# Spreading the second direction's input projection, its convolution and the next image's token embedding over other scan steps

## The chip, the cores and the metric

One core of one Trainium2 chip. The metric is the device time of one launch in microseconds (us), the median of the runs. One execution was taken by the profiler; its trace is what the rows below come from.

## What is computed

For each of 32 images of 224 x 224 x 3 and a text of 77 tokens, one layer of an early-fusion model. T = 1 + 196 + 77 = 274 tokens of C = 192 features.

```python
h = concat([cls, patches(x / 255) @ W + b]) + pos_emb        # 197 tokens, patch length 768
h = concat([h, txt], axis=1)                                  # 274 tokens
h = h + attn(layernorm(h))                                    # two Mamba blocks, forward and backward
h = h + ffn(layernorm(h))                                     # a transformer block

def mamba(x, ...):                        # once on x, once on x reversed in time
    xi, z = split(x @ in_proj.T)          # 384 + 384 features
    xc = silu(causal_dwconv(xi, 4 taps))
    dt_lo, B, C = split(xc @ x_proj.T)    # 12 + 16 + 16
    dt = softplus(dt_lo @ dt_w.T + dt_b)
    h_t = exp(dt_t * A) * h_(t-1) + dt_t * u_t * B_t          # 384 features x 16 states
    y = (h_t . C_t + u * D) * silu(z)
    return y @ out_proj.T
```

The mixer ends in r = x + fwd + bwd and a layernorm. The transformer block has 12 heads of 16 features and an MLP of 768. The first 16 images ("large") go through attention and MLP once; for the last 16 ("small") attention and MLP outputs are gated sums of three variants with masked heads and channels, which costs more matmuls and adds.

## The kernel before

Features lie on partitions, tokens along the free axis; everything is fp32. The five engines each have a program of their own, written by hand, and wait for each other by semaphores. The selective scan is cut into 12 half units per image: q = 0 to 5 is the first direction (d = 0), 6 to 11 the second, each half unit a tile of 128 partitions (16 states x 8 features) by 8 x 274. For each q, VectorE multiplies the loaded dt*u rows with B (`input_product`, L1073), runs one long TENSOR_TENSOR_SCAN (`scan`, L1084) and multiplies with C (`output_product`, L1090); ScalarE makes the decays by eight exps (`exps`, L832); TensorE sums over the states into `y_ps` (`sum_states`, L476 and L480), and VectorE gates the sum (`gate_unit`, L1099). dt and dt*u go through DRAM to be broadcast over partitions: SyncE writes them (`write_rows`) and reads them back (`read_half`) in a fixed order.

The order of all work is a table of gaps. `step(b, f, e, a)` is one turn of the loop: it has 2 x GAPS = 36 gaps, three for each q, and in it four images are under way. Image b is being scanned. Image f = b - 1 goes through output projection, the second layernorm and attention (`fine...` functions, with its own gap count 0 to 35), image e = b - 2 through its MLP and last sum (the same functions, gap count 36 to 45, in the first ten gaps of the step). Image a = b + 1 is prepared (`fronts...` functions). The same gap number on every engine stands for the same place in the schedule, but each engine runs through its own list as its waits allow. In this text gap g of the second direction is also called gap 18 + g.

Fronts, before: in the first half of the step (d = 0) the second direction of image b is prepared, in the second half (d = 1) the first direction of image a. In each half:

- gaps 0 to 5: `in_proj` (L516), six column blocks j of 128, two matmuls each, into the one PSUM bank `a_ps`; ScalarE's `xz_copy` (L855) empties it one gap later, j = 0 to 2 into `xi`, j = 3 to 5 into `zs[d]`.
- VectorE's `conv` (L1138 and L1142, four taps for one j) at CONV_GAPS; ScalarE's `silu` (L860 and L861, between two table loads) at gap 8.
- `x_proj_mm` (L526) and its copy at gap 10; `dt_mm` (L536) with `dt_parts` (L873 to L879, Abs, Relu, Exp, Ln) at gaps 11 to 13, `dt_sum` (L1149 and L1152) on VectorE one gap later; `c_spread` and `c_copy` at 14, `b_spread` at 15.

In the first half also the token embedding of image a: 12 matmuls `tok` (L492, gaps 6 and 7), `tok_add` (L1123, gap 7), the mean over features `a_mean_mm` (L468) and VectorE's `centre` (L1104, gap 8), ScalarE's `squares` (gap 8), `a_var_mm` (L468) and `rstd` (gap 9), and VectorE's `scale_by` that makes `xn` (L1109, gap 10). Everything of the fronts that TensorE makes except B goes through the bank `a_ps`, so its order is a strict sequence of matmuls and copies.

Of the image f, the gaps named below are: `residual` (L1157) at gap 4, which waits for `out_proj` (L556); `add_mixer` at 7; `affine` (L1116) at 10; q, k and v matmuls (L581, L606) at 11 and 12; from gap 12 on 18 slots of scores (L621) with their row maxima on VectorE one gap later (L1178) and turned scores (L629) with their exp on ScalarE (L924); `q_with_maxima` (L595, L598) at 15, 20 and 26; sums of attention inverted on ScalarE (L936, L938) and divided on VectorE (L1183) at 24, 30 and 33; `proj` (L654) at 33. Of image e: fc1 (L675) at gaps 2 and 3, gelu (L951) at 4, fc2 (L686) at 5 and 6, for small images its second and third variant at 8, `add_mlp` (L1187 or L1192) at 7 and `last_sum` (L1187, L1196, L1238) at 9.

How a gap is gone through, here on VectorE:

```python
if gap % 3 == 0: output_product(b, q - 1)
if gap % 3 == 1: scan(b, q)
if gap % 3 == 2: input_product(b, q + 1)
if gap % 6 == 2: gate_unit(b, q // 2 - 1)
for part in endings(d, gap, f, e): fine(*part)
fronts(b, d, a, gap)
```

## Time and profile before

| what | before |
|---|---|
| median of 3 runs | 5700.33 us (5692.26 to 5709.53) |
| the profiled execution | 5727.32 us |
| its span | 5725.5 us |
| VectorE (DVE) busy | 4944.8 us, 86% |
| TensorE (PE) busy | 4406.4 us, 77% |
| ScalarE (ACT) busy | 3172.3 us, 55% |
| DMA, mean of the 16 engines | 72.2% |
| granted TensorE clock, mean | 0.799 |

The span is the stretch from the first to the last instruction that the profiler saw. A timeline row gives start, duration, engine, line, operation, out<-in, shapes and count, and in brackets how long the engine had idled before it and what released it; rows of one kind that follow each other are merged, and on PE the count takes weight loads and matmuls together. The granted clock is a share of 2.4 GHz; 0.5 is the level of 1.2 GHz.

### The profile page before, as it was taken

The numbers are of one execution on the slowest core, as the hardware profiler recorded it, in microseconds if no ns is written. First come the engines' busy times: TensorE is split into PE (matmuls) and PEld (weight loads), VectorE is DVE, ScalarE is ACT, GpSimd is POOL, SyncE is SP. The second block draws the span as 40 slices with busy tenths as digits, with TensorE's granted clock in tenths as the row PEclk, the third lists the DMA queues.
The fourth block names the chain that finished last, engine by engine and source line by source line (L and its number), as shares of the span: only waits on it lengthen the run. The fifth ranks groups of instructions, "written<-read, shape, count | busy, mean of one in ns | idle before, by whom it ended". The sixth has DMA issues, their size and how long they took to land.

```text
span 5725.5 us, 69728 instructions
## 1 busy us (share of the span) xinstructions
PE 4406.4 (77%) x23852; PEld 2476.2 (43%) x23852; DVE 4944.8 (86%) x3712; ACT 3172.3 (55%) x6914; POOL 1.5 (0%) x9
## 2 busy tenths in 40 slices
PE   3577778777777877777778787788778877787877
PEld 2244444444344444444444444444445444444433
DVE  4999998999999899999998988888987889888971
ACT  2455555555565555555556655555555655556642
POOL 0000000000000000000000000000000000000000
PEclk7677888887788878877888878887877878888876
DMA  5877787778778777877786786777766677676840
GB/s 143 206 170 172 175 198 179 177 172 188 178 164 192 182 178 170 194 176 164 178 191 162 168 186 149 165 165 163 169 152 163 159 178 162 155 176 163 178 101 3
DMA packets 182843, 953.92 MB, mean 167 GB/s; under 512 B 26557, under 2 KB 76157, under 8 KB 84042
## 3 DMA queue, kind: packets, MB, share of 16 engines
q1 hardware_dynamic: 182442, 948.83, 72.2%
q8 instruction: 220, 3.60, 0.3%
q14 instruction: 181, 1.48, 0.1%
HBM read 888.14 MB, written 60.60 MB: 166 GB/s over the span
## 4 chain that ended last, share of the span: by engine, by line
PE 37%; DVE 36%; issue 14%; DMA 7%; ACT 5%; DVEq 1%; SPq 0%; ACTq 0%; POOL 0%; POOLq 0%
DVE hs L1084 15%; DVE hs L1090 6%; DVE hs L1073 5%; PE f_ps L675 4%; DMA h<-in_txt 3%; PE a_ps L516 3%; DVE neg_max L1178 3%; PE f_ps L639 3%; PE f_ps L686 2%; PE f_ps L629 2%; PE y_ps L480 2%; PE f_ps L556 2%; PE a_ps L526 2%; PE f_ps L581 2%; DVE xc L1142 2%
## 5 line engine op out<-in xcount | busy, mean ns | idle before, releaser
L1084 DVE TENSOR_TENSOR_SCAN hs<-decay,hs 128x2192 f32<-128x2192 f32 x384 | 1810.5, 4715 | 27.6 <-ACT decay L832 27.5
L832 ACT ACTIVATE decay<-decay,a_cols 128x273 f32<-128x273 f32 x3072 | 1369.0, 511 | 0.4
L1090 DVE TENSOR_TENSOR hs<-hs,c_s 128x2192 f32<-128x2192 f32 x384 | 933.5, 2431 | 56.0 <-issue 56.0
L1073 DVE TENSOR_TENSOR hs<-hs,b_ps 128x2192 f32<-128x2192 f32 x384 | 930.4, 2423 | 17.1 <-DMA hs<-dtu_rows 17.1
L924 ACT ACTIVATE hid<-f_ps 92x1096 f32<-92x1096 f32 x288 | 310.9, 1079 | 649.4 <-PE f_ps L629 649.1
L480 PE MATMUL y_ps<-hs,y_pick 128*32 128x274 f32 x6144 | 554.5, 490 | 55.4 <-DVE hs L1090 55.4
L516 PE MATMUL a_ps<-xn,w_in_s 96*128 96x274 f32 x1536 | 514.6, 463 | 98.0 <-ACT zs L855 50.5
L1178 DVE TENSOR_REDUCE neg_max<-f_ps 92x4 f32<-92x1096 f32 x288 | 371.5, 1290 | 185.9 <-PE f_ps L621 185.9
L629 PE MATMUL f_ps<-hid 32*92 32x274 f32 x1536 | 189.5, 573 | 339.5 <-DVE neg_max L1178 329.8
L516 PEld LDWEIGHTS a_ps<-xn,w_in_s 96*128 96x128 f32 x1536 | 319.2, 219 | 275.7 <-ACT zs L855 77.6
L480 PEld LDWEIGHTS y_ps<-hs,y_pick 128*32 128x32 f32 x6144 | 185.4, 127 | 374.8 <-issue 241.8
L581 PE MATMUL f_ps<-cen,w_qk_s 96*128 96x274 f32 x768 | 257.3, 471 | 90.2 <-DVE cen L1116 55.5
L1142 DVE SCALAR_TENSOR_TENSOR xc<-xi,inner_s,xc 128x274 f32<-128x274 f32 x576 | 289.9, 504 | 20.1
L675 PE MATMUL f_ps<-cen,fc_s 96*128 96x274 f32 (+2 forms) x960 | 292.4, 456 | 4.1 <-DVE cen L1116 3.1
L686 PE MATMUL f_ps<-hid,fc_s 128*96 128x274 f32 x1152 | 287.3, 399 | 7.1 <-ACT hid L951 6.0
L639 PE MATMUL f_ps<-hid,v_s 92*32 92x274 f32 x2304 | 237.3, 567 | 55.4 <-ACT hid L924 33.5
L629 PEld LDWEIGHTS f_ps<-hid 32*92 32x92 f32 x1536 | 64.3, 202 | 451.2 <-DVE neg_max L1178 309.2
L621 PE MATMUL f_ps<-hid 32*92 32x274 f32 x1536 | 169.9, 518 | 86.3 <-ACT hid L924 47.3
L675 PEld LDWEIGHTS f_ps<-cen,fc_s 96*128 96x128 f32 (+2 forms) x960 | 194.5, 212 | 92.2 <-ACT hid L944 30.6
L944 ACT ACTIVATE hid<-f_ps,fc_b_s 128x274 f32<-128x274 f32 x384 | 181.5, 489 | 93.5 <-PE f_ps L675 92.8
L581 PEld LDWEIGHTS f_ps<-cen,w_qk_s 96*128 96x128 f32 x768 | 152.5, 216 | 185.9 <-DVE cen L1116 66.5
L686 PEld LDWEIGHTS f_ps<-hid,fc_s 128*96 128x96 f32 x1152 | 188.2, 165 | 94.5 <-issue 11.5
(149 smaller groups left out, 5927.9 us busy)
## 6 DMA issues: line engine op xcount, KB each, us to landing
decay<-dt_rows SPq DMA_DIRECT2D x384, 1096.0 KB, 9.0
hs<-dtu_rows SPq DMA_DIRECT2D x384, 1096.0 KB, 12.8
dt_rows<-dt SPq DMA_DIRECT2D x192, 137.0 KB, 10.0
dtu_rows<-dtu SPq DMA_DIRECT2D x192, 137.0 KB, 9.8
xp<-in_patches SPq DMA_DIRECT2D x32, 588.0 KB, 19.5
out<-h SPq DMA_DIRECT2D x32, 205.5 KB, 2.2
h<-in_txt SPq DMA_DIRECT2D x32, 57.8 KB, 11.7
w_in_s<-in_w_in SPq DMA_DIRECT2D x1, 1152.0 KB
```

Of the source, the lines that this page charges most:

```text
L480: mm = pe.matmul(y_ps[32 * g:32 * g + 32, 0:T], y_pick[:, 2 * (q % 2) + v, :], hs[q % 4][:, 4 * v + g, :], start=False, stop=(q % 2 == 1 a ...
L516: mm = pe.matmul(a_ps[:, 0:T], w_in_s[:, i, d, j * 128:(j + 1) * 128], xn[parity(b)][:, i, :], start=(i == 0), stop=(i == 1))
L581: mm = pe.matmul(f_ps[:, bank, 0:T], w_qk_s[:, i, s, g * 128:(g + 1) * 128], cen[:, i, :], start=(i == 0), stop=(i == 1))
L639: mm = pe.matmul(f_ps[32 * r:32 * r + 32, AV_BANKS[g], 0:T], v_s[:, k, hd * 2 * HD:(hd + 1) * 2 * HD], prob_t[:, r, k, :], start=(k == 0), ...
L675: mm = pe.matmul(f_ps[:, c, 0:T], fc1_s[rows, i, ch * 128:(ch + 1) * 128], cen[rows, i, :], start=((rows, i) == FC1_ROWS[small][0][0]), st ...
L686: mm = pe.matmul(f_ps[0:CH, VARIANTS[v][2][i], 0:T], fc2_s[:, ch, i * CH:(i + 1) * CH], hid[:, HC * v + ch, :], start=(ch == 0), stop=(ch ...
L832: e = act.activation(dec[:, k, t], dec[:, k, t], ACT.Exp, scale=a_cols[:, d * IC + u, TILES * half + k:TILES * half + k + 1])
L1073: dve.tensor_tensor(x[:, :, :], x[:, :, :], b_ps[:, 0:T].unsqueeze(1).broadcast_to([128, TILES, T]), ALU.mult).then_inc(dbu_done, 1)
L1084: dve.tensor_tensor_scan(i, a, i, 0.0, ALU.mult, ALU.add).then_inc(scan_done, 1)
L1090: dve.tensor_tensor(x[:, :, :], x[:, :, :], c_s[d][:, :].unsqueeze(1).broadcast_to([128, TILES, T]), ALU.mult).then_inc(hc_done, 1)
L1142: dve.scalar_tensor_tensor(out=xc[d][:, j, :], in0=xi[:, j, t:t + T], scalar=w, in1=xc[d][:, j, :], op0=ALU.mult, op1=ALU.add)\
L1178: dve.tensor_reduce(neg_max[:, g % 2, t, :].rearrange("p (r c) -> p r c", r=4)[:, :, HD], f_ps[0:QT, 0:4, 0:T], AX_X, ALU.min).then_inc(nm ...
```

## The change

No instruction's operands change. The table of gaps and the places in `fronts` change:

- The first half (xi, j = 0 to 2) of direction 1's `in_proj` is done a step ahead, at gaps 32 to 34 of the step before (X_AHEAD_GAP = 14 in d = 1), copied at 33 to 35. The second half (zs) is done at gaps 0 to 2.
- Direction 1's convolution is at gaps 1, 3, 5 (was 3, 5, 7), silu at 6 (8), x projection at 7 (10), dt at 8 to 10 (11 to 13), C at 11 (14).
- The token matmuls are at gaps 15 and 16 (6 and 7), the token add at 16 (7), the mean, centring and squares at 17 (8), the variance, rstd and scaling at 18 (9, 9 and 10).
- Direction 0's `in_proj` is at gaps 19 to 24 (18 to 23), its x projection at 27 (28), dt at 28 to 30 (29 to 31), C at 31 (32).
- Waits follow the order: tokens wait for the copy of C, the wait of direction 1's x projection for the next image's Ln goes, the zs copies wait for one gating each, and the first convolution of direction 1 waits until the sums of the image before have read `xc[1]`.
- The front, once, does the three blocks of direction 1 as well.

```diff
-        CONV_GAPS = ((3, 5, 7), (4, 5, 7))
-        XP_GAP = 10
-        DT_GAPS = (11, 12, 13)
-        C_GAP = 14
+        CONV_GAPS = ((1, 3, 5), (4, 5, 7))
+        SILU_GAPS = (6, 8)
+        XP_GAPS = (7, 9)
+        DT_GAPS = ((8, 9, 10), (10, 11, 12))
+        C_GAPS = (11, 13)
         B_GAP = 15
+        X_AHEAD_GAP = 14
+        TOK_GAPS = (15, 16)
+        TOK_ADD_GAP, MEAN_GAP = 16, 17
+        A_VAR_GAP = XN_GAP = 0
...
                 if not first(b):
-                    pe.wait_ge(xz_copied, at(ago(b, 1), 12, 12))
+                    pe.wait_ge(c_copied, at(ago(b, 1), 2, 2))
...
-                if d == 1 and not last(b):
-                    pe.wait_ge(a_ln, at(b, 1, 2))
...
-                x, xd = (b, 1) if d == 0 else (a, 0)
-                if x is not None:
-                    if gap < 2 * IC:
-                        in_proj(x, xd, gap, gap + 1)
-                if d == 0 and a is not None and gap == 6:
+                if d == 0 and gap < IC:
+                    in_proj(b, 1, IC + gap, IC + gap + 1)
+                if d == 0 and a is not None and gap == TOK_GAPS[0]:
                     tok(a, (0,))
+                if d == 1 and a is not None:
+                    if 1 <= gap <= 2 * IC:
+                        in_proj(a, 0, gap - 1, gap)
+                    if 0 <= gap - X_AHEAD_GAP < IC:
+                        in_proj(a, 1, gap - X_AHEAD_GAP, gap - X_AHEAD_GAP + 1)
...
-                    if j == IC:
-                        wait(act, gated, at(ago(b, 1), UNITS, IC * (d + 1)))
+                    if j >= IC:
+                        wait(act, gated, at(ago(b, 1), UNITS, IC * d + j - IC + 1))
...
                         if k == 0:
+                            if d == 1 and j == 0:
+                                wait(dve, ysum, at(b, SCANS, -1))
```

TensorE in the step of the loop over large images, from the scores of gap 15 to those of gap 17, before (`neg_max` are the row maxima, `hs` the scanned states, `hid` and `qk` hold q and k):

```order
L621 MATMUL f_ps<-hid 92x274 x4
L595 MATMUL f_ps<-ident,neg_max 128x92
L595 MATMUL f_ps<-ident,neg_max 128x91 x2
L598 MATMUL f_ps<-cen,w_qk_s 128x274 x2
L476 MATMUL y_ps<-xc,d_diag 128x274
L480 MATMUL y_ps<-hs,y_pick 32x274 x8
L629 MATMUL f_ps<-qk 92x274 x4
L621 MATMUL f_ps<-hid 92x274 x4
```

and now, up to the variance at gap 18 (line numbers are those of the changed file):

```order
L601 MATMUL f_ps<-cen,w_qk_s 128x274 x2
L492 ISA
L497 MATMUL a_ps<-xp,tok_w_s 96x196 x12
L481 MATMUL y_ps<-xc,d_diag 128x274
L485 MATMUL y_ps<-hs,y_pick 32x274 x8
L632 MATMUL f_ps<-qk 92x274 x4
L505 ISA
L473 MATMUL a_ps<-h,mean_w 96x274 x2
L624 MATMUL f_ps<-hid 92x274 x4
L473 MATMUL a_ps<-xp,mean_w 96x274 x2
L632 MATMUL f_ps<-qk 92x274 x4
```

The token matmuls, the mean and the variance have come in between the turned maxima and the scores that VectorE reduces at gap 18.

VectorE in the same loop, from the affine of gap 10 to the scan of gap 13, before:

```order
L1116 TENSOR_SCALAR cen<-cen,feat_s 96x274 x2
L1109 TENSOR_TENSOR xn<-xn,rstd_a 96x548
L1073 TENSOR_TENSOR hs<-hs,b_ps 128x2192
L1090 TENSOR_TENSOR hs<-hs,c_s 128x2192
L1149 TENSOR_TENSOR dt<-dt,dtu 128x274
L1152 TENSOR_TENSOR dtu<-dt,xc 128x274
L1178 TENSOR_REDUCE neg_max<-f_ps 92x4
L1084 SCALAR_TENSOR_TENSOR hs<-decay,hs 128x2192
```

and now:

```order
L1130 TENSOR_SCALAR cen<-cen,feat_s 96x274 x2
L1165 TENSOR_TENSOR dt<-dt,dtu 128x274
L1168 TENSOR_TENSOR dtu<-dt,xc 128x274
L1087 TENSOR_TENSOR hs<-hs,b_ps 128x2192
L1165 TENSOR_TENSOR dt<-dt,dtu 128x274
L1168 TENSOR_TENSOR dtu<-dt,xc 128x274
L1104 TENSOR_TENSOR hs<-hs,c_s 128x2192
L1194 TENSOR_REDUCE neg_max<-f_ps 92x4
L1098 SCALAR_TENSOR_TENSOR hs<-decay,hs 128x2192
```

The scaling of xn has left for gap 18, and two dt sums stand where one stood; the third lies before the scan of gap 10.

## Rows read from the trace of the kernel before

**Rows 1.** The page: the span, and busy time of two engines.
```profile
span 5725.5 us, 69728 instructions
PE 4406.4 (77%) x23852; PEld 2476.2 (43%) x23852; DVE 4944.8 (86%) x3712; ACT 3172.3 (55%) x6914; POOL 1.5 (0%) x9
```
**Rows 2.** Waits of DVE: engine line <- releaser, us in total, times, longest.
```profile
DVE neg_max L1178 <- PE f_ps L621: 185.9, 81, 9.6
DVE o_s L1183 <- ACT f_ps L938: 163.5, 33, 14.2
DVE xn L1104 <- PE a_ps L468: 68.8, 30, 6.0
DVE cen L1157 <- PE f_ps L556: 62.0, 14, 10.6
```
**Rows 3.** Timeline of PE, gaps 11 and 12 of one step with large images.
```profile
1613.28 3.45 PE L581 MATMUL f_ps<-cen,w_qk_s 96*128 96x274 f32 x8 [1.95 <-DVE cen L1116]
...
1621.20 1.12 PE L536 MATMUL a_ps<-dt_lo,dt_w_s 128*128 128x274 f32 x2
1622.25 1.24 PE L621 MATMUL f_ps<-qk 32*92 32x274 f32 x8
```
**Rows 4.** Timeline of ACT, gap 11 of that step.
```profile
1617.67 0.40 ACT L873 ACTIVATE dtu<-a_ps 128x274 f32<-128x274 f32 x1 [6.67 <-PE a_ps L536]
...
1619.14 0.38 ACT L900 ACTIVATE qk<-f_ps 128x274 f32<-128x274 f32 x1
```
**Rows 5.** Timeline of DVE, gaps 12 and 13 of that step.
```profile
1619.27 0.45 DVE L1149 TENSOR_TENSOR dt<-dt,dtu 128x274 f32<-128x274 f32 x1 [0.70 <-ACT dtu L879]
...
1623.73 1.30 DVE L1178 TENSOR_REDUCE neg_max<-f_ps 92x4 f32<-92x1096 f32 x1 [3.44 <-PE f_ps L621]
```
**Rows 6.** Timeline of DVE, gaps 4 to 9 of one step with small images.
```profile
4702.41 0.72 DVE L1157 TENSOR_TENSOR cen<-f_ps,xn 96x548 f32<-96x548 f32 x1 [2.36 <-PE f_ps L556]
...
4711.91 4.72 DVE L1084 TENSOR_TENSOR_SCAN hs<-decay,hs 128x2192 f32<-128x2192 f32 x1 [1.58 <-ACT decay L832]
...
4727.91 0.72 DVE L1104 TENSOR_TENSOR xn<-h,a_ps 96x548 f32<-96x548 f32 x1 [3.20 <-PE a_ps L468]
...
4730.90 1.03 DVE L1187 SCALAR_TENSOR_TENSOR res<-f_ps,gate,res 96x274 f32<-96x274 f32 x2
```
**Rows 7.** Timeline of PE, gaps 6 to 8 of that step.
```profile
4716.94 4.14 PE L492 MATMUL a_ps<-xp,tok_w_s 128*96 128x196 f32 x24
...
4727.71 2.94 PE L686 MATMUL f_ps<-hid,fc_s 128*96 128x274 f32 x12
```
**Rows 8.** Timeline of ACT, gaps 4 and 5 of that step.
```profile
4709.65 1.28 ACT L952 ACT_TABLE_LOAD   x1
4710.94 0.93 ACT L832 ACTIVATE decay<-decay,a_cols 128x273 f32<-128x273 f32 x2
```
**Rows 9.** Timeline of DVE, gap 17 of the large step.
```profile
1644.52 2.41 DVE L1073 TENSOR_TENSOR hs<-hs,b_ps 128x2192 f32<-128x2192 f32 x1
```
**Rows 10.** Timeline of PE, gaps 15 and 16 of the large step.
```profile
1636.46 0.71 PE L621 MATMUL f_ps<-hid 32*92 32x274 f32 x8 [1.67 <-DVE neg_max L1178]
...
1637.88 2.09 PE L598 MATMUL f_ps<-cen,w_qk_s 96*128 96x274 f32 x4
...
1642.05 0.71 PE L629 MATMUL f_ps<-qk 32*92 32x274 f32 x8
```
**Rows 11.** Line 492, all its matmuls: duration ns min/median/max, first and last start.
```profile
L492 PE MATMUL a_ps<-xp,tok_w_s x768: 327/329/621, 40.8 to 5253.1; 128*96 128x196 f32 x192
```
**Rows 12.** Stretches of the large step: us, busy PE, PEld, DVE, ACT, POOL, clock, DMA share, GB/s.
```profile
1625.00:1635.00 10.00, 8.64 (x54) 4.68 (x54) 9.93 (x9) 6.70 (x18) 0.00 (x0) 1.00 1.01 226
1635.00:1640.00 5.00, 3.54 (x19) 2.67 (x20) 5.00 (x5) 0.51 (x2) 0.00 (x0) 0.78 1.04 228
```
**Rows 13.** Timeline of PE, gap 16 of the small step.
```profile
4768.06 2.06 PE L480 MATMUL y_ps<-hs,y_pick 128*32 128x274 f32 x16
```
**Rows 14.** Timeline of DVE, gap 30 of the large step.
```profile
1703.19 0.44 DVE L1183 TENSOR_TENSOR o_s<-o_s,f_ps 128x274 f32<-128x274 f32 x1 [5.14 <-ACT f_ps L938]
```

More of the change, by code:

```diff
@@ L742, in fronts @@
             def fronts(b, d, a, gap):
[L744 to L749 removed]
+                if d == 0 and gap < IC:
+                    in_proj(b, 1, IC + gap, IC + gap + 1)
+                if d == 0 and a is not None and gap == TOK_GAPS[0]:
+                    tok(a, (0,))
+                if d == 1 and a is not None:
[3 more added lines that the diff above has]
+                        in_proj(a, 1, gap - X_AHEAD_GAP, gap - X_AHEAD_GAP + 1)
             def fronts_early(b, d, a, gap):
                 x, xd = (b, 1) if d == 0 else (a, 0)
[L752 removed]
+                if x is not None and gap == XP_GAPS[d]:
                     x_proj_mm(x, xd)
[L754 to L756 removed]
+                if x is not None and gap in DT_GAPS[d]:
+                    dt_mm(x, xd, DT_GAPS[d].index(gap))
+                if x is not None and gap == C_GAPS[d]:
                     c_spread(x, xd)
@@ L760, in fronts_early @@
                 if d == 0 and a is not None:
-                    if gap == 7:
+                    if gap == TOK_GAPS[1]:
                         tok(a, (1,))
-                    if gap == 8:
+                    if gap == MEAN_GAP:
                         a_mean_mm(a)
-                    if gap == 9:
-                        a_var_mm(a)
+                if d == 1 and a is not None and gap == A_VAR_GAP:
+                    a_var_mm(a)
             def step(b, f, e, a):
@@ L804, in front @@
                 b_spread(b, 0)
+                in_proj(b, 1, 0, IC)
             def finish(f, e):
@@ L1049, in front @@
                 c_copy(b, 0)
+                xz_copy(b, 1, 0, IC)
                 act.wait_ge(s_ac, 1)
@@ L1275, in fronts @@
                         conv(x, xd, (CONV_GAPS[d].index(gap),))
-                    if gap - 1 in DT_GAPS:
-                        dt_sum(x, xd, DT_GAPS.index(gap - 1))
+                    if gap - 1 in DT_GAPS[d]:
+                        dt_sum(x, xd, DT_GAPS[d].index(gap - 1))
                 if d == 0 and a is not None:
-                    if gap == 7:
+                    if gap == TOK_ADD_GAP:
                         tok_add(a)
-                    if gap == 8:
+                    if gap == MEAN_GAP:
                         centre(h[parity(a)], xn[parity(a)], a_ps[0:CH, 0:T], a_mean, at(a, 1, 1), a_cen)
-                    if gap == 10:
-                        scale_by(xn[parity(a)], xn[parity(a)][:, :, :], rstd_a, a_rstd, at(a, 1, 1), xn_ready)
+                if d == 1 and a is not None and gap == XN_GAP:
+                    scale_by(xn[parity(a)], xn[parity(a)][:, :, :], rstd_a, a_rstd, at(a, 1, 1), xn_ready)
             def step(b, f, e, a):
```

27 lines of the change are left out of this document (14 added, 13 removed).

## The prediction

> **What bounds the kernel now.** I read the page first. VectorE is busy for 4944.8 of 5725.5 us, TensorE for 4406.4, and VectorE is the only engine above 80% [rows 1]. The change adds no VectorE instruction and takes none away, so it can only win what VectorE idles, 780 us, less the start before the first scan (96 us) and the drain of the last two images. Next, the waits of VectorE in total [rows 2]: the row maxima wait for the scores on TensorE (185.9 us), the division of the attention sums for ScalarE (163.5), the centring of the next image for TensorE's mean (68.8), the residual for the output projection (62.0). Last, the timeline of single steps. A step starts with scan 0; I count gaps 0 to 17 of the first direction and 18 to 35 of the second. Steps up to the 17th take about 165 us, with 10 to 15 us idle; from the 18th (the image two back is of the second half) 172 to 187, with 15 to 30 idle.
>
> **Term 1, the first row maximum (gap 13), in 31 steps.** What sets it is not VectorE's own queue but a chain through TensorE and ScalarE that starts at the affine of gap 10. The q/k matmuls start at 1613.28 and end at 1616.7; the first dt matmul follows; ScalarE does four dt activations, 1617.67 to 1619.14, and only then the copies of q, k and v; TensorE then does a v matmul, the second dt matmul from 1621.20 to 1622.25, and the scores [rows 3, 4]. VectorE reaches the dt sum 0.70 early and the maximum 3.44 early [rows 5]. After the change direction 1's dt parts lie at gaps 8 to 10, and at gap 11 there is one C matmul and its single copy. A single copy takes 0.38 us, the four 1.47: 1.1 us earlier. The second dt matmul is gone: 1.05. The scores come 2.1 us earlier. VectorE's own work between affine and maximum hardly moves: the scaling of xn (0.65) and one dt sum (0.9) go out, two dt sums (1.7) come in. So 2.1 of the 4.1 us idle go, 31 x 2.1 = **-65 us**. Bounds: nothing (the late parts only move), and all of it, 4.1 x 31 = -127.
>
> **Term 2, gaps 1 to 9 of the 13 steps from the 18th.** VectorE waits 2.36 for the output projection, 1.58 for decay and 3.20 for the mean [rows 6]. The first shrinks because one convolution (2.0 us) moves from gap 7 to gap 1 in front of it; TensorE's side does not depend on it. The last disappears from here: token matmuls (4.14 us), mean and variance (0.93 each) leave this stretch [rows 7]. But then the next thing late is the third gated MLP part at gap 9, whose matmuls end at 4730.6 behind all that [rows 7]. I place it again. ScalarE's two decays after the table load at 4709.65 end at about 4711.4 (one zs copy fewer before), squares 11.9, three decays 13.4, rstd 14.4, then the silu, which is now here at gap 6: table load 1.28 and 0.89, so direction 1's x projection starts at 4716.5. TensorE: 1.5, states 1.1, MLP part two 2.85, centring 1.85, dt 0.65, MLP part three 2.8: done at 4727.3. VectorE has nothing left from about 4723.9 and waits 3.4. Its add comes at 4727.4 where it came at 4731.4 (half of the pair at 4730.90): 4.0 earlier, of which 1.1 is the token add and centring that have moved. 13 x 2.9 = **-38 us**. Bounds 0 and, all three waits gone, 13 x 7.1 = -92.
> The row of ScalarE's table switch shows 1.28 us and the next activation straight behind it (4709.65, 4710.94) [rows 8]. The Trainium skill (ScalarE: Activation LUTs, "What ACT_TABLE_LOAD costs") gives 2.66 us for a switch, a drain included; by that the x projection would be 1.4 us later and the sum some 18 us worse, about 5657. The trace disagrees with the page, and I go by the row.
>
> **Term 3, the same centring wait in the earlier steps.** It is 0.2 to 3.4 us there, 26 us in all of the 68.8 (13 x 3.2 = 42 are in term 2). TensorE no longer owes a mean at gap 8, and the text half of the image, which is loaded only after gap 4, has landed long before gap 17: **-26 us**.
>
> **Term 4, the new place: gaps 15 to 18, 31 steps.** Here the trace of before has no wait at all [rows 9], and the change puts one chain in. From the end of the maximum of gap 15 (1636.4), VectorE has output product, maximum and scan, 8.1 us, before the token add, then 0.5 and an input product of 2.35 before the centring. TensorE has scores, turned maxima and q (1636.46 to 1640.0, 3.6 us) [rows 10], then the new 12 token matmuls, then states, turned scores and the mean. A token matmul takes 0.33 us, the longest 0.62 [rows 11]; 12 take 4.14 in one go. At full clock: tokens end at 7.7, the mean at 7.7 + 1.8 + 0.7 + 1.0 = 11.2, VectorE arrives at 11.0: 0.2. But the granted clock is 0.78 where the tokens would come in this step, partly the 1.2 GHz level [rows 12], and in 21 of 31 steps the q matmul there takes 2.0 or so instead of 1.12; in a later step the eight state matmuls behind it are at half speed too (2.06 where they mostly take 1.13) [rows 13]. With the first 6 to 8 token matmuls at half speed they end near 9.7: 1.6 of waiting at the token add, 0.7 at the mean. One third at 0.2, two thirds at 2.3, and 0.3 for the maximum of gap 18 that now waits for scores behind the mean, and 0.3 for xn, which has 3.5 us of cover for squares, variance, Ln and Exp (0.6 + 1.0 + 0.9, behind three decays of 1.5): about 2.2 us. 31 x 2.2 = **+68 us**. Bounds: 0.5 x 31 = +15, and everything at half speed (rival one). Nothing refunds it, VectorE is the engine that waits.
>
> **Terms at nothing.** Direction 0's x projection and dt parts come one gap earlier (27 to 30) in front of the attention sums: 0.65 us more in front of the division at gap 30, which waits 5.14 [rows 14], but a dt sum of 0.9 now lies before it. In-projection of direction 1, first half, at gaps 32 to 34: 3 x 1.09 us on TensorE, hidden by its wait for the last division; if that cover is gone, 31 x 1 us. Its copies and the convolution find their data a step ahead. The new wait of the first convolution on the states of scan 10 is met a gap and a scan earlier. The loads keep SyncE's order; dt rows are ready earlier, which only helps. The front gains three projections behind which the first decay waits for its DMA anyway.
>
> **Sum.** -65 - 38 - 26 + 68 = -61 us against the profiled execution's 5727.3, so 5666. That execution is 27 us above the median of the runs, 5700.3; from the median the same difference gives **5640**. I call a difference under 0.3% (17 us) no change; more than that a measurement can tell.
>
> **Rivals.** *One, slower: the token matmuls run at half speed where VectorE has no cover.* Twelve at 0.62 are 7.5 us, so they end at 11.1 and the token add waits 3.0; states, turned scores and mean at half take 6.2 against 2.85: 3.4 more; maximum and xn 1.1. That is 7.5 x 31 = +232, less 129 of gains: 5803. It decides from a new wait of 4.2 us a step. For it: rows 12 and 13. Against it: clock 1.00, the 2.4 GHz level, in the ten microseconds before [rows 12], a recovered 0.71 for turned scores at 1642.05 [rows 10], and the token matmuls themselves fill a stretch in which TensorE idled. The Trainium skill (TensorE: Matmul & The Clock Gate, "What's actually happening") says that the default state is throttled and that activity releases it; work moved from a stretch where TensorE never pauses into one with pauses would by that rule be at half rate, and this rival is its time. The rows bear it out in part.
> *Two, no change:* term 1 moves along with its chain, or term 4 comes to about 4 us; the gains of the three terms are 129 and are given back at gaps 16 and 17: 5700.
> *Three, more:* the whole wait of gap 13 goes and TensorE is at full clock at gap 15: -127 - 38 - 26 + 15 = -176, 5524.
> That the change does not do what it says is out: the order of instructions shows the token matmuls behind the q matmul of gap 15.
>
> **Chances.** Forecast 0.58 (own range 5600 to 5680), more gain 0.14, no change 0.13, slower 0.15. A small part of the forecast lies within 0.3%: faster 0.71, same 0.14, slower 0.15. The range leaves out the ends of both outer rivals and takes a mild form of the first: 5550 to 5735.
>
> **What would show it.** Right: no wait of the centring at gap 8, the first maximum waits about 2 us instead of 4.1 with the dt sum's, a wait of 3 us before the gated add at gap 9 in late steps, and a new group of waits of about 2 us a step on the token add, the mean and the maximum of gap 18; VectorE idles about 60 us less. Wrong: token add and mean waiting over 4 us a step with a clock near 0.5; or the wait of the division at gap 30 growing by more than 1 us, which would mean that ScalarE's dt parts now stand in front of it.

## The result and the profile after: slower, where faster was forecast

| what | before | after |
|---|---|---|
| median of the runs | 5700.55 us | 5772.06 us (5754.98 to 5773.32) |
| profiled execution | 5727.32 us | 5771.23 us |
| VectorE (DVE) busy | 4944.8 us | 4946.4 us |
| TensorE (PE) busy | 4406.4 us | 4647.7 us |
| granted TensorE clock, mean | 0.799 | 0.765 |

The ratio of the runs is 1.0118, with a 95% interval of 1.0094 to 1.0143 (the quotient of the two medians is 1.0125; all ratios below are of this kind and differ from quotients of medians by up to 0.2%): the change costs 1.2%, some 70 us. The forecast was 5640, and the range ended at 5735. The median of before is now from four runs, hence 5700.55 where the prediction had 5700.33. The profiled execution of before is 27 us above its median and that of after 1 us below its own, so the two traces are only 44 us apart.

The page of after, its span, busy times and the clock over 40 slices; [rows 1] answer to the first two lines:

```profile
span 5769.4 us, 69870 instructions
PE 4647.7 (81%) x23852; PEld 2587.6 (45%) x23852; DVE 4946.4 (86%) x3712; ACT 3167.4 (55%) x6914; POOL 1.5 (0%) x9
PEclk7677778777777877777777777777778777787876
```

The number of matmul records, 23852, is the same. An fp32 matmul of the program leaves two MATMUL records and two weight-load records (the 12 token matmuls of an image are 24 of each in the trace); so the counts on PE in all rows, those before the prediction too, are two for each matmul, and not weight loads and matmuls together. The same matmuls keep TensorE busy for 241 us more. Nothing was added, so they ran slower: the mean clock fell from 0.799 to 0.765. VectorE's work is the same within 2 us; its idle time grew by 42. Its waits in the trace of after (line, releaser, us in total, times, longest), to be read against [rows 2]:

```profile
DVE neg_max L1194 <- PE f_ps L624: 321.1, 104, 9.6
DVE res L1203 <- PE f_ps L689: 100.0, 26, 29.9
DVE cen L1173 <- PE f_ps L559: 84.0, 17, 11.1
DVE dt L1165 <- ACT dtu L887: 73.8, 34, 12.5
DVE hs L1104 <- issue: 44.0, 11, 5.7
DVE o_s L1199 <- ACT f_ps L946: 44.0, 33, 13.5
DVE h L1137 <- PE a_ps L497: 20.9, 9, 8.4
DVE xn L1123 <- ACT rstd_a L853: 10.7, 13, 3.8
DVE xn L1118 <- PE a_ps L473: 3.8, 8, 1.3
DVE hs L1098 <- ACT decay L840: 2.2, 3, 1.0
```

The row maxima waited 185.9 us for scores and now wait 321.1. The division fell from 163.5 to 44.0 and the centring from 68.8 to 3.8, yet the sum is a loss. Summed by place over the 31 steps (from VectorE's timeline of all steps, each wait put to the scan that it follows), us. These rows are +52 together; the waits after scan 11 are 7 less:

| place | before | after | forecast of the difference |
|---|---|---|---|
| after scan 3: first maximum, its dt sum, the next maximum (gaps 13, 14) | 125 | 116 | -65 (term 1) |
| centring at gap 8, steps before the 18th | 25.9 | 0 | -26 (term 3) |
| late steps, gaps 1 to 9 | 124.5 | 104.4 | -38 (term 2) |
| after scan 5: token add, mean, maximum of gap 18, xn | 0 | 25 | +68 (term 4) |
| after scan 6: maxima of gaps 20 and 22 | 32 | 155 | none |
| gap 30: division and dt sum | 139 | 79 | 0 |
| residual at gap 4, steps before the 18th | 0.5 | 19 | none |

The row that was in no term is the largest: +123 us at gaps 20 to 22, where neither VectorE's instructions nor the order of TensorE's from the maximum of gap 20 on changed.

**What is slow there.** TensorE in the large step before, gaps 18 to 22 (timeline: start, duration, engine, line, operation; the count is of records, two for each matmul):

```profile
1648.19 1.23 PE L629 MATMUL f_ps<-qk 32*92 32x274 f32 x8 [3.35 <-DVE neg_max L1178]
...
1653.47 1.24 PE L621 MATMUL f_ps<-hid 32*92 32x274 f32 x8
...
1656.36 0.71 PE L629 MATMUL f_ps<-qk 32*92 32x274 f32 x8 [0.44 <-DVE neg_max L1178]
1657.01 0.90 PE L595 MATMUL f_ps<-ident,neg_max 92*128 92x92 f32 x6
1657.75 1.12 PE L598 MATMUL f_ps<-cen,w_qk_s 96*128 96x274 f32 x4
1658.71 1.09 PE L516 MATMUL a_ps<-xn,w_in_s 96*128 96x274 f32 x4
1659.73 1.59 PE L639 MATMUL f_ps<-hid,v_s 92*32 92x274 f32 x24
1661.25 0.71 PE L621 MATMUL f_ps<-hid 32*92 32x274 f32 x8
```

and in the same step after, from gap 15 on:

```profile
1822.29 4.14 PE L497 MATMUL a_ps<-xp,tok_w_s 128*96 128x196 f32 x24
...
1829.97 0.71 PE L624 MATMUL f_ps<-hid 32*92 32x274 f32 x8 [0.24 <-ACT hid L932]
1832.32 2.05 PE L473 MATMUL a_ps<-xp,mean_w 96*96 96x274 f32 x4 [1.64 <-ACT xp L847]
1834.31 1.24 PE L632 MATMUL f_ps<-qk 32*92 32x274 f32 x8
...
1842.00 0.71 PE L632 MATMUL f_ps<-qk 32*92 32x274 f32 x8 [1.91 <-DVE neg_max L1194]
1842.64 1.59 PE L598 MATMUL f_ps<-ident,neg_max 92*128 92x92 f32 x6
1844.03 2.09 PE L601 MATMUL f_ps<-cen,w_qk_s 96*128 96x274 f32 x4
1845.91 2.03 PE L521 MATMUL a_ps<-xn,w_in_s 96*128 96x274 f32 x4
1847.88 2.97 PE L642 MATMUL f_ps<-hid,v_s 92*32 92x274 f32 x24
1850.78 1.24 PE L624 MATMUL f_ps<-hid 32*92 32x274 f32 x8
```

The chain from the maximum of gap 20 to the scores that the maximum of gap 22 reduces is the same in both: turned scores and maxima, q, a block of projection, the attention sums, scores. Before it takes 5.6 us (1656.36 to 1661.96), after 10.0 (1842.00 to 1852.02). The clock of the two stretches (us, busy PE, PEld, DVE, ACT, POOL, granted clock, DMA share, GB/s), first before, gaps 18 and 19 and then 20 to 22:

```profile
1648.00:1652.00 4.00, 3.81 (x20) 1.83 (x24) 4.00 (x3) 2.43 (x5) 0.00 (x0) 0.50 0.98 217
1655.00:1662.00 7.00, 6.56 (x59) 3.80 (x58) 6.35 (x5) 4.11 (x10) 0.00 (x0) 1.00 0.97 212
```

then after, at about gap 16, at gap 18, in the stretch between, and at gaps 20 to 22:

```profile
1824.00:1828.00 4.00, 4.00 (x37) 2.96 (x39) 4.00 (x2) 0.20 (x1) 0.00 (x0) 1.00 0.31 79
1832.00:1836.00 4.00, 3.68 (x20) 1.57 (x24) 3.64 (x3) 2.75 (x8) 0.00 (x0) 0.55 1.01 226
1840.00:1844.00 4.00, 2.09 (x15) 1.61 (x15) 4.00 (x3) 1.48 (x2) 0.00 (x0) 0.83 0.55 127
1842.00:1852.00 10.00, 10.00 (x55) 5.50 (x55) 4.99 (x3) 4.22 (x10) 0.00 (x0) 0.53 1.01 224
```

Before, TensorE idles 3.35 us until 1648.19 and falls to the 1.2 GHz level for gaps 18 and 19, where VectorE has scans and products and does not need it; by 1655 it is back at 2.4 GHz. After, in this step, the token matmuls run in gaps 15 and 16 at the full 2.4 GHz and the idle is 1.64 us around 1831. The clock is at the 1.2 GHz level from 1832.4 to 1839.2, back at 2.4 GHz until 1842.6 (the 0.83 of the third row), and low again from there to 1856.3. This second low stretch is the new one. It begins just as the chain does, behind an idle of 1.91 us, where before the block of projection ended 0.44 us ahead of the chain. VectorE pays for it (timeline of DVE before, then after):

```profile
1662.20 1.30 DVE L1178 TENSOR_REDUCE neg_max<-f_ps 92x4 f32<-92x1096 f32 x1 [0.85 <-PE f_ps L621]
```

```profile
1852.25 1.30 DVE L1194 TENSOR_REDUCE neg_max<-f_ps 92x4 f32<-92x1096 f32 x1 [5.26 <-PE f_ps L624]
```

Over the steps (the first left out) the interval between scan 6 and scan 7 shows it too. Before, 28 of 30 take 13.0 us at a clock of 0.80 to 0.90, and two take 16.4 at 0.62. After, all take 15.9 to 17.9, at 0.50 to 0.70. Placed against the start of scan 6, the clock before is 0.50 in all 30 steps from 2 us ahead of it to 2 us behind it, and 1.00 in 28 of them from 6 to 12 us behind it, where the chain lies. After, it is 0.50 in all 30 from 7 to 12 us behind it. In 18 of these steps it had come back to 1.00 in between, as in the step above; in the other 12, all from the 18th on, it was low the whole way.

### The profile page after: what moved, and what is told of

It is laid out like the page before. It is cut to its first block, busy times and chain, and to the rows that moved or that the text cites. A ratio compares the mean times of both kernels' runs of the same rounds, so it can differ in the third digit from the quotient of the medians.

```text
span 5769.4 us, 69870 instructions
## 1 busy us (share of the span) xinstructions
PE 4647.7 (81%) x23852; PEld 2587.6 (45%) x23852; DVE 4946.4 (86%) x3712; ACT 3167.4 (55%) x6914; POOL 1.5 (0%) x9
## 4 chain that ended last, share of the span: by engine, by line
PE 38%; DVE 35%; issue 16%; ACT 8%; DMA 1%; DVEq 1%; SPq 0%; ACTq 0%; POOL 0%; POOLq 0%
DVE hs L1098 14%; DVE hs L1087 5%; DVE hs L1104 5%; PE f_ps L678 4%; PE f_ps L584 3%; DVE neg_max L1194 3%; PE f_ps L642 3%; PE a_ps L521 3%; PE y_ps L485 2%; DVE xc L1158 2%; PE f_ps L601 2%; PE f_ps L689 2%; PE f_ps L609 2%; PE f_ps L559 2%; PE f_ps L624 2%
## 5 line engine op out<-in xcount | busy, mean ns | idle before, releaser
L1087 DVE TENSOR_TENSOR hs<-hs,b_ps 128x2192 f32<-128x2192 f32 x384 | 931.3, 2425 | 15.2 <-DMA hs<-dtu_rows 14.8
L1194 DVE TENSOR_REDUCE neg_max<-f_ps 92x4 f32<-92x1096 f32 x288 | 371.6, 1290 | 321.1 <-PE f_ps L624 321.1
L485 PE MATMUL y_ps<-hs,y_pick 128*32 128x274 f32 x6144 | 594.9, 513 | 62.4 <-DVE hs L1104 33.7
L521 PE MATMUL a_ps<-xn,w_in_s 96*128 96x274 f32 x1536 | 596.7, 524 | 50.8 <-ACT zs L863 39.0
L521 PEld LDWEIGHTS a_ps<-xn,w_in_s 96*128 96x128 f32 x1536 | 370.9, 253 | 252.5 <-issue 86.5
L632 PE MATMUL f_ps<-hid 32*92 32x274 f32 x1536 | 173.1, 527 | 309.4 <-DVE neg_max L1194 272.4
L584 PE MATMUL f_ps<-cen,w_qk_s 96*128 96x274 f32 x768 | 301.5, 537 | 104.3 <-DVE cen L1130 69.5
L689 PE MATMUL f_ps<-hid,fc_s 128*96 128x274 f32 x1152 | 300.7, 413 | 8.9 <-ACT hid L959 7.7
L584 PEld LDWEIGHTS f_ps<-cen,w_qk_s 96*128 96x128 f32 x768 | 179.1, 253 | 224.6 <-DVE cen L1130 94.0
L539 PE MATMUL a_ps<-dt_lo,dt_w_s 128*128 128x274 f32 x384 | 150.1, 476 | 101.4 <-ACT dt L883 100.2
```

Of the source, the lines that this page charges most:

```text
L485: mm = pe.matmul(y_ps[32 * g:32 * g + 32, 0:T], y_pick[:, 2 * (q % 2) + v, :], hs[q % 4][:, 4 * v + g, :], start=False, stop=(q % 2 == 1 a ...
L521: mm = pe.matmul(a_ps[:, 0:T], w_in_s[:, i, d, j * 128:(j + 1) * 128], xn[parity(b)][:, i, :], start=(i == 0), stop=(i == 1))
L584: mm = pe.matmul(f_ps[:, bank, 0:T], w_qk_s[:, i, s, g * 128:(g + 1) * 128], cen[:, i, :], start=(i == 0), stop=(i == 1))
L689: mm = pe.matmul(f_ps[0:CH, VARIANTS[v][2][i], 0:T], fc2_s[:, ch, i * CH:(i + 1) * CH], hid[:, HC * v + ch, :], start=(ch == 0), stop=(ch ...
L1087: dve.tensor_tensor(x[:, :, :], x[:, :, :], b_ps[:, 0:T].unsqueeze(1).broadcast_to([128, TILES, T]), ALU.mult).then_inc(dbu_done, 1)
L1194: dve.tensor_reduce(neg_max[:, g % 2, t, :].rearrange("p (r c) -> p r c", r=4)[:, :, HD], f_ps[0:QT, 0:4, 0:T], AX_X, ALU.min).then_inc(nm ...
```

## The experiments

My theory after this reading, A: the token matmuls, mean and variance at gaps 15 to 18 bring TensorE's low clock onto gaps 20 to 22. The rivals: the loss comes from the other part of the change, the projections done a step ahead; or gaps 20 to 22 wait for more work in TensorE's queue and the clock only goes with it. Experiments 1 to 3 take the change apart, 4 to 9 test the clock, 10 and 11 put the pieces together. Experiments 1 to 4 share one set of runs of before (median 5722.87 us on that chip), 5 to 8 a second (5725.45), 9 to 11 a third (5718.4); compare ratios. Each is one kernel, timed in three rounds.

**1. The tokens alone.** Only the token work and direction 0's projection are at their new gaps. Against the changed kernel (the projections of direction 1 stay within its own step, too):

```diff
-        CONV_GAPS = ((1, 3, 5), (4, 5, 7))
-        SILU_GAPS = (6, 8)
-        XP_GAPS = (7, 9)
-        DT_GAPS = ((8, 9, 10), (10, 11, 12))
-        C_GAPS = (11, 13)
-        X_AHEAD_GAP = 14
+        CONV_GAPS = ((3, 5, 7), (4, 5, 7))
+        SILU_GAPS = (8, 8)
+        XP_GAPS = (10, 10)
+        DT_GAPS = ((11, 12, 13), (11, 12, 13))
+        C_GAPS = (14, 14)
```

> The kernel before with one part of the change: tokens, mean, variance and xn at gaps 15 to 18, and with them direction 0's projection at 19 to 24 (one gap later). dt, convolution and the other projection stay. Theory A (the token move alone shifts TensorE's low clock onto gaps 20 to 22): the maxima after scan 6 wait 120 us or more in all (32 before, 155 after), the clock from scan 6 to 7 falls to about 0.6, time 5750 to 5800. Theory B (the loss comes of the early dt parts and projections, which thin out TensorE's work ahead of it): waits after scan 6 stay under 60 us, time 5640 to 5690, since the mean's 65 us are won and the tokens cost under 30.

5814.43 us, ratio 1.0178 (1.0142 to 1.0213). Its waits of VectorE:

```profile
DVE neg_max L1188 <- PE f_ps L624: 300.8, 102, 9.6
DVE o_s L1193 <- ACT f_ps L943: 159.4, 33, 13.5
```

The waits after scan 6 are 155.6 us, as with the whole change, at a clock of 0.65 and 0.68 there (steps before and from the 18th); the division keeps its wait. The time is above the 5750 to 5800 that theory A allowed. So the loss at gaps 20 to 22 comes with this part alone. But the part is two moves: direction 0's projection, one gap later, leaves one block fewer ahead of the chain, and in this trace TensorE idles 1.1 to 3.7 us there, where before it was at most 1.3. No run has the tokens moved and that projection left, so which of the two does it was not shown.

**2. The projections ahead alone.** The changed kernel with the token work, direction 0's projection, and both directions' silu, x projection and dt parts back in place. The projections of direction 1 stay a step ahead, its convolution at gaps 1, 3 and 5:

```diff
-        TOK_GAPS = (15, 16)
-        TOK_ADD_GAP, MEAN_GAP = 16, 17
-        A_VAR_GAP = XN_GAP = 0
+        TOK_GAPS = (6, 7)
+        TOK_ADD_GAP, MEAN_GAP = 7, 8
+        A_VAR_GAP, XN_GAP = 9, 10
...
-                    if 1 <= gap <= 2 * IC:
-                        in_proj(a, 0, gap - 1, gap)
+                    if gap < 2 * IC:
+                        in_proj(a, 0, gap, gap + 1)
...
-        SILU_GAPS = (6, 8)
-        XP_GAPS = (7, 9)
-        DT_GAPS = ((8, 9, 10), (10, 11, 12))
-        C_GAPS = (11, 13)
+        SILU_GAPS = (8, 8)
+        XP_GAPS = (10, 10)
+        DT_GAPS = ((11, 12, 13), (11, 12, 13))
+        C_GAPS = (14, 14)
```

> The kernel before with the other part alone: direction 1's first three projections a step ahead at gaps 32 to 34, its other three at 0 to 2, convolution at 1, 3, 5. Tokens, silu and dt where they were. Theory A: waits after scan 6 stay at 30 to 40 us; the residual's wait of late steps falls by up to 2 us a step, 5670 to 5700. Theory B: part of the loss shows here, waits after scan 6 over 60 us and time over 5710.

5754.42 us, ratio 1.0073 (1.0048 to 1.0098). After scan 6 it waits 28.6 us, which clears it of that place. But it is slower than before, where a gain was expected; of theory B the time came true and the wait after scan 6 did not. The new waits are the token add at 24 us (0 before), the adds of the attention's projection after scan 11 at 29 (2.5 before) and, in the early steps, the residual at gap 4 at 15 (0.5 before). The last is the 19 us of the table: it comes from this part, since experiment 1 has 0.7 there. The wait for the mean is still 70 us (67.5 before): with the tokens at gaps 6 to 8 it has no cover. So the tokens' move, with direction 0's projection, costs 1.8% alone, the projections ahead 0.7%, and the whole change, with the earlier x projection and dt parts, 1.2%.

**3. Direction 1's dt parts late again.** The changed kernel but for

```diff
-        XP_GAPS = (7, 9)
-        DT_GAPS = ((8, 9, 10), (10, 11, 12))
-        C_GAPS = (11, 13)
+        XP_GAPS = (10, 9)
+        DT_GAPS = ((11, 12, 13), (10, 11, 12))
+        C_GAPS = (14, 13)
```

> The changed kernel with direction 1's x projection, dt and C back at gaps 10, 11 to 13 and 14; all else as changed. Theory A: waits after scan 6 stay near 155 us, time within 20 us of the changed kernel's, 5750 to 5795. Theory B: TensorE has its dt matmuls between gaps 11 and 14 again, its clock from scan 3 to 4 rises to 0.7 and the waits after scan 6 fall under 100, time 5700 to 5745.

5770.9 us, ratio 1.0084 (1.0048 to 1.012), the same as the changed kernel within the intervals. What term 1 had taken for the largest gain of the change, direction 1's dt parts out of gaps 11 and 12, is worth nothing that can be measured while the clock is as it is. The trace shows why: around gap 13 (maxima and dt sum after scans 3 and 4) the waits are 127 us instead of 116, but the gated add at gap 9 waits 18.5 instead of 47.9. The early dt parts win 11 us at one place and lose 29 at the other. They also lower the clock between scans 3 and 4: it is 0.80 and 0.75 here (steps before and from the 18th) and 0.61 and 0.64 in the changed kernel. And with the clock back up there, the waits after scan 6 are still 159 us, which goes against theory B. The waits of gap 30 stay at 19.9 (division) and 58.6 (dt sum), as after the change: that gain is direction 0's, whose x projection and dt parts come one gap earlier.

**4 and 5. Needless matmuls where TensorE idles.** The changed kernel, with matmuls whose result nobody reads put into TensorE's waits at gap 18 and gap 20. Experiment 4 has 1 and 3, experiment 5 has 2 and 5. Nothing else moves; the two waits in front of them are on things due there anyway (experiment 9 tries them alone). In number 5 (in number 4 the counts are 1 and 3; gap counts within a direction here, 0 and 2 of d = 1 being 18 and 20):

```diff
+            def warm(n, sem_, value, x):
+                pe.wait_ge(sem_, value)
+                for _ in range(n):
+                    pe.matmul(a_ps[:, 0:T], w_in_s[:, 0, 0, 0:128], xn[parity(x)][:, 0, :], start=True, stop=True)
...
+                if d == 1 and a is not None and gap == 0:
+                    warm(2, a_cen, at(a, 1, 1), b)
+                if d == 1 and a is not None and gap == 2:
+                    warm(5, xz_copied, at(a, 12, 1), b)
```

> The changed kernel with matmuls that nobody needs, where TensorE idles: one at gap 18 before the variance, three at gap 20 before the turned scores, all into the free bank a_ps. No result depends on them. Clock theory: the low clock from scan 6 to 7 is a matter of TensorE's idle time just before, so with 124 matmuls more the clock there rises from 0.60 to 0.8, the waits after scan 6 fall from 155 us to under 80, and the time to 5680 to 5740. Queue theory (TensorE is late there because the tokens put more work in front, at whatever clock): the waits after scan 6 stay or grow by 0.5 to 1.5 us a step, time 5770 to 5820.

5693.69 us, ratio 0.9965 (0.9948 to 0.9982). The interval after scan 6 takes 13.0 to 13.2 us in 14 steps, all with a clock of 0.88 or more, and 16.0 to 17.9 in the other 16, with 0.65 to 0.79. Three fifths of the wait are left, 94.5 us, where under 80 was expected: these few fillers do not reach every step. The 19 us of the residual at gap 4 in the early steps are gone as well.

> As e4_fill_18_20, with two needless matmuls at gap 18 and five at gap 20 (before one and three). Clock theory: more steps keep the clock through gaps 20 to 22; the steps whose stretch from scan 6 to 7 takes 13.0 us rise from 14 of 30 to 20 or more, waits after scan 6 fall from 94 us to 60, though the fillers may hold up the turned scores by up to 1 us a step; time 0 to 40 us under e4's. Queue theory: 217 us of chip work more in front of the attention chain shows as 30 us or more over e4.

5598.25 us, ratio 0.9786 (0.9732 to 0.984). Waits of the row maxima in all, then TensorE and VectorE in the same step, gaps 20 to 22, and the granted clock:

```profile
DVE neg_max L1203 <- PE f_ps L624: 177.2, 102, 9.7
```

```profile
1791.48 2.58 PE L760 MATMUL a_ps<-xn,w_in_s 96*128 96x274 f32 x10 [0.49 <-ACT xi L872]
1794.56 0.71 PE L632 MATMUL f_ps<-qk 32*92 32x274 f32 x8 [0.51 <-DVE neg_max L1203]
...
1799.44 0.71 PE L624 MATMUL f_ps<-hid 32*92 32x274 f32 x8
...
1800.39 1.30 DVE L1203 TENSOR_REDUCE neg_max<-f_ps 92x4 f32<-92x1096 f32 x1 [0.84 <-PE f_ps L624]
```

```profile
1788.60:1801.60 13.00, 12.01 (x94) 7.20 (x86) 12.15 (x7) 7.48 (x19) 0.00 (x0) 1.00 0.86 189
```

L760 is the filler: five matmuls, ten records. The chain takes 5.6 us again (1794.56 to 1800.15), the wait is 0.84 as before the change, and all 30 intervals take 13.0 us at a clock of 1.00. The waits after scan 6 fall from 155 to 25 us. More matmuls, and the kernel is 3.3% faster than the changed one (0.9786 against 1.0118). By the ratios it ends some 100 us below experiment 4, where 40 at most were expected. The 217 in the expectation is the number of fillers, not their time; at 0.52 us each (2.58 for five) they are some 112 us of TensorE.

**6 and 7. The same at other places.** Experiment 6 is number 4 with 6 more fillers at gap 4 and 6 at gap 26, in the changed kernel; 7 is the kernel before the change with 6 at gap 26 and none elsewhere.

```diff
+                if d == 0 and gap == 4:
+                    warm(6, xz_copied, at(b, 12, 12), b)
...
+                if d == 1 and a is not None and gap == 8:
+                    warm(6, xz_copied, at(a, 12, 6), b)
```

> As e4_fill_18_20, with six more at gap 4, where TensorE waits for the residual, and six at gap 26, where it idles 4 us before the turned scores (clock 0.53 to 0.57 there). Clock theory: the stretch from scan 8 to 9 rises to 0.8 or more, x projection, sums and dt of gaps 27 to 30 come earlier, and the waits after scan 9 (79 us in the changed kernel) fall under 45; the time falls 30 to 80 us under e4's. If instead those waits come from the chain of ScalarE's copies and not from the rate of the matmuls, they stay and the time is e4's within 15 us.

5606.7 us, ratio 0.9816 (0.9774 to 0.9859), against 0.9965 without them. The clock between scans 8 and 9 rises to 0.79 from 0.53 and 0.57 (early and late steps of the changed kernel), and the waits at gap 30 fall from 79 to 16 us. Not all of the gain is gap 26's: the first maximum waits 61 us where it waited 86 in experiment 4. The waits after scan 6 are not better, 112 against 94.5.

> The kernel before, unchanged but for six needless matmuls at gap 26. There the clock is 0.54 to 0.58 and the division at gap 30 waits 139 us in all. Clock theory: the clock from scan 8 to 9 rises to 0.8, the waits after scan 9 fall to 60 to 90 us, time 40 to 80 us under the kernel before. Rival (the chain there is ScalarE's): no change within 15 us.

5638.2 us, ratio 0.9852 (0.9806 to 0.9898): the division's wait of 138.8 us at gap 30 of the kernel before, most of the second largest of [rows 2], falls to 2.7, where 60 to 90 were expected, and the clock between scans 8 and 9 rises from 0.57 and 0.54 to 0.79 and 0.75. The wait had the name of ScalarE's activation in the profile, yet it went when TensorE was held at the higher level. In this kernel a new wait of 44.5 us came up for the scaling by ScalarE's `rstd_f` after scan 0. Neither here nor at gaps 4 and 10 was the wait in front of the fillers tried alone.

**8. Gap 10.** Experiment 4 with four fillers more at gap 10, into the buffer that holds the projection's output until then:

```diff
+                        if (d, gap) == (0, 10) and e is not None:
+                            pe.wait_ge(out_ready, at(e[0], 1, 1))
+                            for _ in range(4):
+                                pe.matmul(f_ps[:, 0, 0:T], w_in_s[:, 0, 0, 0:128], xn[parity(b)][:, 0, :],
+                                          start=True, stop=True)
```

> As e4_fill_18_20, with four needless matmuls at gap 10 before q and k, into a free bank. In the changed kernel the stretch from scan 3 to 4 takes 14.5 us where the clock is 0.72 or more (7 of 30 steps) and 18.2 where it is 0.53 to 0.67. Clock theory: the clock there rises over 0.7, most steps take 14.5 to 15.5, and the time falls 50 to 90 us under e4's; this is the gain that my term 1 had counted on. Queue theory: four matmuls in front of the q matmuls delay the chain by 0.5 to 1.5 us a step, and the time rises by 15 to 50 us over e4's.

5590.75 us, ratio 0.9763 (0.9714 to 0.9812), against 0.9965: some 115 us, where 50 to 90 were expected. The clock between scans 3 and 4 is 0.75 and 0.95, and the maximum of gap 13 now waits 38 us in all, where it was 91 with the changed kernel (41.6 before the 18th step, 49.2 from there). The gain of term 1 exists once TensorE's clock is held up.

**9. The control.** The waits of experiments 4 and 5 with no matmul behind them:

```diff
-                    warm(2, a_cen, at(a, 1, 1), b)
+                    warm(0, a_cen, at(a, 1, 1), b)
...
-                    warm(5, xz_copied, at(a, 12, 1), b)
+                    warm(0, xz_copied, at(a, 12, 1), b)
```

> Control for e5_fill_more: the changed kernel with its two added waits of TensorE (for the centring at gap 18, for the first xi copy at gap 20) and none of its seven matmuls. Clock theory: it is the matmuls' activity that counts, so the clock from scan 6 to 7 stays at 0.57 to 0.65, the waits after scan 6 near 155 us, and the time is the changed kernel's within 20 us. Rival (the two waits only shift the order of events so that the engines fit better): the gain of e5_fill_more, 100 us or more, appears here too.

5777.37 us, ratio 1.0109 (1.0092 to 1.0125): the changed kernel's time. Waits of its row maxima:

```profile
DVE neg_max L1203 <- PE f_ps L624: 332.5, 102, 9.7
```

It is the matmuls, not the waits in front of them, that bring the gain.

**10 and 11. All together, and the fair comparison.** Number 10 has 6, 4, 2, 5 and 6 fillers at gaps 4, 10, 18, 20 and 26 of the changed kernel; number 11 has 4 at gap 10 and 6 at gap 26 of the kernel before. Number 10 against number 8:

```diff
+                if d == 0 and gap == 4:
+                    warm(6, xz_copied, at(b, 12, 12), b)
...
-                    warm(1, a_cen, at(a, 1, 1), b)
+                    warm(2, a_cen, at(a, 1, 1), b)
...
-                    warm(3, xz_copied, at(a, 12, 1), b)
+                    warm(5, xz_copied, at(a, 12, 1), b)
...
+                if d == 1 and a is not None and gap == 8:
+                    warm(6, xz_copied, at(a, 12, 6), b)
```

> The changed kernel with all fillers: six matmuls at gap 4, four at 10, two at 18, five at 20, six at 26. If the gains of the single places add (gaps 18 and 20 some 130 us over the changed kernel, gap 10 some 80, gaps 4 and 26 some 80), waits after scan 6 are 25 us, after scan 3 under 45, after scan 9 under 25, and the time is 5460 to 5540. If they overlap, since the granted clock of one stretch depends on the one before, 5540 to 5590.

5473.36 us, ratio 0.9578 (0.9562 to 0.9594). The page and its waits:

```profile
span 5468.2 us, 72730 instructions
PE 4506.1 (82%) x25282; PEld 2633.5 (48%) x25282; DVE 4940.5 (90%) x3712; ACT 3157.7 (58%) x6914; POOL 1.5 (0%) x9
PEclk7789899989899898989899897888889878888876
```

```profile
DVE neg_max L1212 <- PE f_ps L624: 126.8, 84, 9.7
DVE o_s L1217 <- ACT f_ps L964: 30.4, 13, 13.5
```

TensorE does 715 matmuls more than in the changed kernel (1430 records) and is busy 142 us less. This version beats both kernels, the one before by 4.2%.

> The kernel before with the two fillers that fit its order: four matmuls at gap 10, six at gap 26. It shows which of the two orders is better once TensorE's clock is held. If the change is sound and only the clock spoiled it, this one ends 40 to 100 us above e9_fill_all: 5560 to 5620. If the order of before is as good, 5480 to 5540.

5555.71 us, ratio 0.9722 (0.9683 to 0.9761). So with the clock held up in both, the changed order is 82 us better than the old one. The two do not have their fillers at the same places, since the old order keeps its clock at gaps 20 to 22 by itself; the 82 us compare two orders each with help where it was found to lack it, not two equal sets. In the traces the old order still waits 70 us for the mean at gap 8, 23 for decay in late steps and 97 at gaps 13 and 14; the new one waits 0, 4 and 53 there, and 22 at its own gaps 16 to 18.

## Why the prediction was wrong, point by point

**What failed.** The step is the one behind all four terms: that TensorE's durations in the trace of before also hold after it. Term 4 looked at the clock at gaps 15 to 18 alone and ended its account at the maximum of gap 18; the stretch behind it was put at nothing without a reason. Before, the low stretch was at gaps 18 and 19, behind TensorE's wait of 3.35 us, where it cost nothing, and the clock was back for the chain of gaps 20 to 22. After, the chain was at 1.2 GHz in every step, in 18 of 30 by a second fall as it began: +123 us in no term. Experiment 1 shows that the token move, with direction 0's projection a gap later, does it, experiment 5 that the clock is the means (130 us of waits gone with needless work), and the control that the waits are not.

**Term 1, -65.** Measured: -9 over gaps 13 and 14. The chain through TensorE has its fewer instructions as worked out, but it ran at a lower clock: 0.61 instead of 0.74 between scans 3 and 4 in the early steps, 0.64 instead of 0.79 in the late ones. By experiment 3 that is the doing of the term's own move, the dt parts that left this stretch. With four fillers at gap 10 in both orders the waits there are 97 us in the old and 42 in the new (experiments 11 and 8, which differ in their other fillers), a gain of 55. The gap 11 step of after shows q/k in 4.02 us where [rows 3] have 3.45:

```profile
1797.04 4.02 PE L584 MATMUL f_ps<-cen,w_qk_s 96*128 96x274 f32 x8 [0.92 <-DVE cen L1130]
1800.99 1.28 PE L545 MATMUL a_ps<-dt_lo,spread 32*128 32x274 f32 x2
...
1805.81 1.24 PE L624 MATMUL f_ps<-qk 32*92 32x274 f32 x8
1807.19 1.30 DVE L1194 TENSOR_REDUCE neg_max<-f_ps 92x4 f32<-92x1096 f32 x1 [3.84 <-PE f_ps L624]
```

Where that stretch happened to have a clock of 0.72 or more, in 7 steps, the interval took 14.5 to 15.2 us; in the other 23, 17.4 to 18.3.

**Term 2, -38.** Measured: -20. The waits for decay (26.0 to 2.2) and for the mean (41.6 to 0) went as worked out. The gated add took back 39 (9.2 to 47.9), as forecast: 3.4 us in 13 steps, 44 in all. What it missed is the residual, which it had let shrink and which grew from 47.7 to 54.3.

**Term 3, -26.** Right: 25.9 to 0.

**Term 4, +68.** Measured at its own place: +25, nearly all of it in the steps before the 18th. The tokens mostly ran at 2.4 GHz, as the row of all 768 records shows beside [rows 11]:

```profile
L497 PE MATMUL a_ps<-xp,tok_w_s x768: 327/329/642, 42.0 to 5346.9; 128*96 128x196 f32 x192
```

The median is all but the minimum. In 8 of the 31 steps some 12 of the 24 records were at the slow level, and the twelve matmuls took 5.9 to 6.2 us instead of 4.1; the token add waited in these 8 steps and in no other, 12.5 us in all. So the mechanism of the slow start is there, but the weight of two thirds was too much (about one quarter), and the term's end was too early.

**Terms at nothing.** Gap 30 was put at nothing and gained 60: the division's wait went from 139 to 20, and a dt sum took over 59 of it. The dt sum in the large step, to be read beside [rows 14]:

```profile
1890.10 0.45 DVE L1165 TENSOR_TENSOR dt<-dt,dtu 128x274 f32<-128x274 f32 x1 [2.01 <-ACT dtu L887]
...
1891.77 0.44 DVE L1199 TENSOR_TENSOR o_s<-o_s,f_ps 128x274 f32<-128x274 f32 x1 [0.65 <-ACT f_ps L946]
```

The 5.14 us are now 2.66. The prediction had named the opposite as a sign against itself, a division that waits longer. Experiment 3 ties the gain to direction 0's earlier parts; by which step of the chain they win was not tried, and the clock between scans 9 and 10 is higher too, 0.85 instead of 0.73.

**The room.** Of VectorE's 780 us idle the stretch before the first scan holds 69, not its full length of 96, and the last step 160.

**The rivals.** Rival one had the right mechanism (TensorE at 1.2 GHz where VectorE has no cover) and the right sign, at 0.15, but the wrong place: gaps 15 to 18 at +232 where they came to +25, nothing for the stretch behind, and 5803 for 5772, which is near by luck. (Its 7.5 us for twelve slow matmuls is also short: a record of [rows 11] is half a matmul and overlaps the next one, so twice 4.14 us is 8.3.) The sentence of the Trainium skill that it cited (TensorE: Matmul & The Clock Gate, "What's actually happening": throttled by default, released by activity) agrees with experiments 5 and 9: needless matmuls, which are activity and nothing else, lift the clock between scans 6 and 7 to 1.00, and the same waits without them leave it at 0.60 and 0.56 (early and late steps). I had applied it to the moved work itself, and what counted was the work behind it. On the table switch of term 2 the prediction says that the trace disagrees with the Trainium skill (ScalarE: Activation LUTs, "What ACT_TABLE_LOAD costs"), and that goes too far: the page splits its 2.66 us into a load of about 1283 ns, which the 1.28 us of [rows 8] bear out, and a drain of about 1380 ns, of which the rows show nothing. Rival two would have had to end within 17 us of no change, and rival three needed all of gap 13's wait to go; neither came.

**The signs.** The test named for wrong, token add and mean over 4 us a step with a clock near 0.5, did not come, nor did a longer wait of the division; and the change lost all the same. A test for every stretch whose clock the moved work could alter could have found it: the low stretch at gaps 18 and 19 stood in the trace of before, just ahead of the chain that then ran at the low level.

**What stays open.** Whether the tokens or direction 0's later projection lower the clock at gaps 20 to 22. Why part two alone costs 0.7%: several small waits, named in experiment 2, were not taken apart. And what exactly, in TensorE's pattern of idle and busy, sends the clock down at one place and not at another: the runs show that filling certain waits lifts it and that 1 and 3 matmuls do in half the steps what 2 and 5 do in all.

## What to carry to other kernels

Where the granted clock is not 1.00, do not take a matmul's duration as fixed: when work of TensorE is moved, find in the trace of before each stretch at 1.2 GHz that costs nothing, and ask which chain that VectorE waits for lies behind the moved work and could come to run at that level. A wait that the profile puts down to another engine can still go back to TensorE's low clock (the division at gap 30). Where TensorE idles just ahead of a chain that VectorE waits for, a few needless matmuls in the idle are a cheap test, and here also the best version.
